# Exponentials as the stationary operand of the value products in a five-stream transformer kernel

## The reference

```
attn = jax.nn.softmax(jnp.einsum('bhqd,bhkd->bhqk', q, k) * scale, axis=-1)
out  = jnp.einsum('bhqk,bhkd->bqhd', attn, v).reshape(B, Lq, H)
x    = x + gate * (out @ Wp + bp)
```

## Time and profile before

| | |
|---|---|
| median of 3 runs | 2109.46 us (2109.4 to 2112.23) |
| profiled execution | 2114.21 us, span 2112.3 us |
| PE busy | 1954.2 us, 93% |
| PE weight loads busy | 1598.7 us |
| DVE busy | 1719.4 us, 81% |
| ACT busy | 1319.1 us, 62% |
| POOL busy | 832.2 us, 39% |
| mean granted TensorE clock | 0.988 of full speed |

### The profile page before, as it was taken

How to read it: one execution, slowest core, us unless ns; L and a number is a source line. 1 busy time by engine, 2 the same in 40 slices (tenths; PEclk the granted TensorE clock), 3 DMA queues, 4 the chain that set the end, 5 groups by cost and what they waited for, 6 DMA issues and landing times.

```text
span 2112.3 us, 93901 instructions
## 1 busy us (share of the span) xinstructions
PE 1954.2 (93%) x40741; PEld 1598.7 (76%) x40741; DVE 1719.4 (81%) x4395; ACT 1319.1 (62%) x3500; POOL 832.2 (39%) x1452
## 2 busy tenths in 40 slices
PE   3788999999999999999999999999999999999998
PEld 3566777787777787777787777887877877877777
DVE  2678788888788888789888889888889888889875
ACT  1344666676666676666666665676766666675666
POOL 1332343444343444343434343434443444344333
PEclk9899999999999999999999999999999999999999
DMA  4200000000000000000000000000000000000000
GB/s 164 56 2 3 15 20 21 8 16 20 21 20 21 8 18 18 21 20 21 8 21 18 18 21 21 20 9 20 18 18 21 21 20 8 21 15 8 3 3 14
DMA packets 48118, 43.01 MB, mean 20 GB/s; under 512 B 12640, under 2 KB 38368, under 8 KB 47456
## 3 DMA queue, kind: packets, MB, share of 16 engines
q1 hardware_dynamic: 47712, 37.02, 6.2%
HBM read 32.54 MB, written 4.46 MB: 18 GB/s over the span
## 4 chain that ended last, share of the span: by engine, by line
PE 60%; DVE 29%; issue 4%; ACT 3%; POOL 2%; DMA 1%; DVEq 0%; ACTq 0%; POOLq 0%
PE bank L975 9%; DVE top L1068 7%; PE bank L866 6%; PE bank L848 5%; PE bank L882 5%; PE bank L870 5%; DVE n_rows L1037 4%; PE bank L895 4%; PE bank L922 4%; DVE inv_sum L1072 4%; PE bank L912 4%; PE bank L905 3%; PE bank L786 3%; PE bank L819 3%; DVE q_heads L1059 2%
## 5 line engine op out<-in xcount | busy, mean ns | idle before, releaser
L724 POOL TENSOR_TENSOR shifted<-moments,eps 128x2 f32<-128x2 f32 x256 | 50.9, 199 | 1046.7 <-DVE moments L1031 1046.0
L1203 ACT ACTIVATE pT<-bank 128x512 f32<-128x512 f32 x640 | 330.4, 603 | 177.6 <-PE bank L870 177.3
L1068 DVE TENSOR_REDUCE top<-bank 128x8 f32<-128x512 f32 x640 | 394.7, 678 | 43.5 <-PE bank L848 42.0
L1072 DVE RECIPROCAL inv_sum<-bank 128x256 f32<-128x256 f32 x160 | 279.6, 1748 | 43.1 <-PE bank L882 42.9
L866 PE MATMUL bank<-inv_sum,of_keys 32*128 32x128 f32 x5120 | 278.9, 286 | 8.0 <-ACT inv_sum L1161 5.9
L870 PE MATMUL bank<-q_heads,k_heads 32*128 32x128 f32 x5120 | 262.7, 273 | 1.4 <-issue 1.1
L1037 DVE TENSOR_SCALAR n_rows<-x_rows,moments,rstd 128x128 f32<-128x128 f32 x512 | 198.4, 429 | 52.8 <-POOL rstd L726 52.1
L866 PEld LDWEIGHTS bank<-inv_sum,of_keys 32*128 32x128 f32 x5120 | 208.4, 188 | 40.8 <-ACT inv_sum L1161 26.5
L1238 ACT ACTIVATE pT<-bank,mod 128x64 f32<-128x64 f32 x896 | 194.7, 334 | 52.6 <-PE bank L975 51.5
L1180 ACT ACTIVATE k_heads<-bank,key_bias,own_head_sb 128x256 f32<-128x256 f32 x320 | 163.3, 563 | 96.6 <-PE bank L823 95.2
L870 PEld LDWEIGHTS bank<-q_heads,k_heads 32*128 32x128 f32 x5120 | 210.0, 189 | 2.5 <-issue 2.4
(11 more groups left out here) (147 smaller groups left out, 4044.4 us busy)
## 6 DMA issues: line engine op xcount, KB each, us to landing
gates<-gate_store SPq DMA_DIRECT2D x64, 256.0 KB, 4.1
x_rows<-x SPq DMA_DIRECT2D x32, 128.0 KB, 2.1
c_rows<-context SPq DMA_DIRECT2D x32, 128.0 KB, 2.1
out<-x_rows SPq DMA_DIRECT2D x32, 128.0 KB, 1.9
w_sb<-weights SPq DMA_DIRECT2D x1, 2368.0 KB, 12.8
pT<-weights SPq DMA_DIRECT2D x1, 1024.0 KB, 4.9
logit_bias<-logit_store SPq DMA_DIRECT2D x64, 1.5 KB, 3.4
row_sb<-rows SPq DMA_DIRECT2D x1, 769.5 KB, 6.8
```

The costliest lines, as they stand in the source:

```text
L1068: nc.vector.tensor_reduce(top[s][:, 32 * g:32 * g + 2 * GROUP], by_turn[g][:, :].rearrange("p (c k) -> p c k", k=SEQ), AX.X, ALU.max).then ...
L1072: nc.vector.reciprocal(inv_sum[s][:, :], banks.take()[:, 0:TOK]).then_inc(v_emptied, 1)
L1203: nc.scalar.activation(turn_cols[s][:, g, :], by_turn[g][:, :], ACT.Exp, scale=ATT_SCALE).then_inc(scores_read, 1)
```

## The change

1. **values**: pT becomes the stationary operand, 32 queries at a time (128x32), and two heads' v_heads of 9 columns each, 18 in all, move past it. Column 9 is all ones, so a head's sum stands beside its 8 outputs. 64 matmuls in the four column tiles instead of 32, and the step **sums** is gone. The matmuls of a turn wait for that turn's exponentials alone. Outputs have queries on the partitions.
2. DVE takes 128x32 reciprocals and multiplies them, broadcast over 8 features, into o_rows. A new step **heads** follows: PE transposes o_rows (two transposes, ring bank for ACT) and ACT moves them into oT.
3. **tops**: the four banks are one PSUM tensor; one TENSOR_REDUCE of 128x2048 waits for the last matmul of the step.
4. v_heads is written by two ACT copies of 64 partitions x 256 instead of four of 128.
5. The context's rows are normed by ACT, as c_rstd * c - mean * c_rstd (two ACTIVATEs of 128x128 with both operands by partition); POOL makes both norms' factors at once. POOL's expert-bias mix takes four wider instructions instead of ten.
6. low and the small attention's p3 and pn3 lie in o_rows instead of inv_sum, one DMA (own_ones) goes, and SEQUENCE is another string of the same length.

```diff
-    return [..., ("scores", None), ("sums", None), ("values", None), ("out", a)]
+    return [..., ("scores", None), ("values", None), ("heads", None), ("out", a)]
...
-        v_heads = each("v_heads", [D, GROUP * TURNS, 2 * QUAD])
+        v_heads = each("v_heads", [D, 2 * GROUP * TURNS, 2, HD + 1])
+        o_rows = each("o_rows", [D, 2, D])
+        inv_sum = each("inv_sum", [D, 2 * HEADS])
...
@@ PE
-                    if kind == "sums":
-                        after("pT", s)
-                        for lo in range(2):
-                            for g in range(TURNS):
-                                mm = nc.tensor.matmul(dst[QUAD * g:QUAD * (g + 1), 0:TOK], own_ones[:, lo, :], pT[s][:, g, :, lo, :],
-                                                      start=lo == 0, stop=lo == 1)
-                    if kind == "values":
-                        after("pT", s)
-                        for tb in range(GROUP):
-                            for lo in range(2):
-                                for g in range(TURNS):
-                                    mm = nc.tensor.matmul(dst[QUAD * g:QUAD * (g + 1), tb * SEQ:(tb + 1) * SEQ],
-                                                          v_heads[s][:, tb * TURNS + g, lo * QUAD:(lo + 1) * QUAD], pT[s][:, g, tb, lo, :],
-                                                          start=lo == 0, stop=lo == 1)
+                    if kind == "values":
+                        for g in range(TURNS):
+                            pe.wait_ge(scores_read, ready["pT", s] + g + 1)
+                            for t in range(2):
+                                for lo in range(2):
+                                    for b in range(2):
+                                        for half in range(2):
+                                            tb, at = 2 * t + b, SEQ * b + 32 * half
+                                            mm = nc.tensor.matmul(dst[at:at + 32, t, g, :, lo, :], pT[s][:, g, tb, lo, 32 * half:32 * half + 32],
+                                                                  v_heads[s][:, 2 * (tb * TURNS + g) + lo, :, :], start=True, stop=True)
+                    if kind == "heads":
+                        after("o_rows", s)
+                        transpose2(to_a.slot(), lambda t: o_rows[s][:, t, :], a_filled)
@@ DVE
-                        for g in range(TURNS):
-                            nc.vector.tensor_reduce(top[s][:, 32 * g:32 * g + 2 * GROUP], by_turn[g][:, :].rearrange("p (c k) -> p c k", k=SEQ), AX.X, ALU.max)
+                        nc.vector.tensor_reduce(top[s][:, :].rearrange("p (g c) -> p g c", c=32)[:, :, 0:2 * GROUP],
+                                                turns[:, :, :].rearrange("p g (c k) -> p g c k", k=SEQ), AX.X, ALU.max)
-                        nc.vector.reciprocal(inv_sum[s][:, :], banks.take()[:, 0:TOK])
-                        nc.vector.tensor_tensor(oT[s]..., src[:, 0:TOK], inv_sum[s][:, :], ALU.mult)
+                        own_result(nc.vector.reciprocal(inv_sum[s][:, :], src[:, :, HD]))
+                        nc.vector.tensor_tensor(o_cols[s]..., src[:, :, 0:HD], inv_sum[s][:, :].unsqueeze(2).broadcast_to([D, 2 * HEADS, HD]), ALU.mult)
@@ ACT
+                        for t in range(2):
+                            m = nc.scalar.activation(cn_rows[s][:, t, :], c_rows[s][:, t, :], ACT.Identity,
+                                                     scale=c_rstd[s][:, e, t:t + 1], bias=c_minus[s][:, e, t:t + 1])
+                    if kind == "heads":
+                        move(oT[s][:, :, :], bank4(banks.take()))
```

More of the change, by code:

```diff
@@ L134, in attention @@
     return [("q", a), ("k", a), ("v", a), ("tops", None), ("lows", None), ("scores", None),
-            ("sums", None), ("values", None), ("out", a)]
+            ("values", None), ("heads", None), ("out", a)]
 def mlp(m):
@@ L220, in bank_uses @@
         "kvnorm": (1, 0) if modulated else (0, 1), "q": (1, 0), "k": (0, 1), "v": (0, 1),
-        "lows": (0, 1), "sums": (1, 0), "values": (1, 0),
+        "lows": (0, 1), "values": (1, 0), "heads": (0, 1),
         "out": (1, 0), "fc1": (0, 1), "fc2": (1, 0), "l3_query": (0, 1), "l3_scores": (1, 0),
@@ L434, in build @@
         logit_store = nc.dram_tensor("logit_store", (B, EXPERTS), F32, kind="Internal").ap()
-        bank = [ctx.enter_context(nc.psum_tensor(f"bank{i}", [D, 512], F32)) for i in range(8)]
+        bank = [ctx.enter_context(nc.psum_tensor(f"bank{i}", [D, 512], F32)) for i in range(4)]
+        turns = ctx.enter_context(nc.psum_tensor("turns", [D, TURNS, 512], F32))
+        bank += [turns[:, g, :] for g in range(TURNS)]
         first_sem = sem("weights_in")
@@ L462, in build @@
         rows_normed, c_normed = [sem(f"rows_normed{s}") for s in range(STREAMS)], [sem(f"c_normed{s}") for s in range(STREAMS)]
-        c_moments_in = sem("c_moments_in")
+        c_moments_in, c_scaled = sem("c_moments_in"), [sem(f"c_scaled{s}") for s in range(STREAMS)]
         n_modulated = sem("n_modulated")
@@ L556, in _ @@
                 nc.gpsimd.memset(eps[:, TIGHT, :], 1e-6).then_inc(consts_made, 1)
-                nc.gpsimd.memset(minus_half[:, :], -0.5).then_inc(consts_made, 1)
+                nc.gpsimd.memset(minus_halves[:, :, :], -0.5).then_inc(consts_made, 1)
                 for s in range(STREAMS):
-                    nc.gpsimd.memset(v_heads[s][:, :, :], 0.0).then_inc(consts_made, 1)
+                    nc.gpsimd.memset(v_heads[s][:, :, :, :], 0.0).then_inc(consts_made, 1)
+                for s in range(STREAMS):
+                    pool.wait_ge(consts_made, 3 + STREAMS + 2 * s)
+                    for pair in range(2):
+                        nc.gpsimd.memset(v_heads[s][SEQ * pair:SEQ * (pair + 1), :, pair, HD:HD + 1], 1.0).then_inc(consts_made, 1)
             @block.tensor
@@ L1187, in _ @@
                             part = slice(SEQ * pair, SEQ * (pair + 1))
-                            for lo in range(2):
-                                at = lo * QUAD + (2 * pair + lo) * HD
-                                m = nc.scalar.activation(v_heads[s][part, :, at:at + HD],
-                                                         src[part, 0:TOK].rearrange("p (n l d) -> p n l d", l=2, d=HD)[:, :, lo, :],
-                                                         ACT.Identity)
+                            m = nc.scalar.activation(v_heads[s][part, :, pair, 0:HD],
+                                                     src[part, 0:TOK].rearrange("p (n d) -> p n d", d=HD), ACT.Identity)
                         m.then_inc(a_emptied, 1)
```

166 lines of the change are left out of this document (78 added, 88 removed).

## The result

| | before | changed |
|---|---|---|
| median | 2110.85 us (4 runs) | 2164.6 us (4 runs, 2161.56 to 2172.44) |
| ratio | 1 | 1.0256, 95% interval 1.0222 to 1.0289 |
| span of the profiled execution | 2112.3 us | 2159.6 us |

The change makes the kernel 2.6% slower; 1991 us was forecast. The page of the changed kernel answers to the earlier trace rows. The last line is the queue that carries instructions: packets, MB, share of 16 engines.

The account below looks back on a forecast made before the run. PE was taken to bound the kernel, with DVE close behind. From 2114.2 us, -88 for PE's products and -30 for waits gave 1996, and the median's 4.7 us lower made 1991 us; the 8 in 10 range was 1920 to 2075.

Parts of the forecast that it names:

- Part 1, products: PE's products with the exponentials: 1.12 us plus 0.22 for transposes replace 1.89 an attention, -88 us over 160.
- The rule that a load waits for the running matmul of its tile: Rival on PE's products: weight loads do not overlap their own tile's matmul, 77 us more, 2068 us; chance 0.06.
- wrong if L884 takes over 1.3 us an attention: Sign on the products' line: 128 records were expected in 1.0 to 1.1 us; over 1.3 refutes the forecast.
- Parts 2 and 3: Engine loads: DVE falls from 1719 to about 1480 us, ACT rises from 1319 to about 1470; neither counts by itself.
- Part 4: POOL loses 105.5 us of context rows and narrows its expert mix; PE waits for it almost nowhere, costed at nothing.
- Part 5: PE's waits: DVE's relief up to -75 us, late exponentials up to +86; -30 taken.
- D: Rival, tight exponentials: half of the 0.54 us is lost (43 us) and DVE's waits stay; 2064 us, chance 0.16.
- E: Rival: PE stands at each first product for late exponentials, 86 us, plus 38 for table loads; 2145 us, chance 0.06.
- The 0.54 us: Before the products: PE's wait an attention for the last turn's exponential, due at 2.4 us; 86 us over 160.
- B: Rival: DVE was a second bound; all 75 us of waits go and half as much again; 1909 us, chance 0.20.
- the sixth, no change: Rival: no change within what can be told, products at +37 us with DVE's waits gone; chance 0.02.
- the far end: Upper price of the products on PE: 14 ns a record, 1.79 us for 128, +37 us over 160 attentions.

Follow-up runs that it names:

- after_onewait: The changed kernel, but the products wait once for all four exponentials instead of turn by turn; 2260.9 us, 1.071 of the kernel before.
- wide_reciprocals: after_wide with 128x256 reciprocals as before the change, giving DVE 1.4 us an attention more; 2251.5 us, 1.065 of the kernel before.
- after_wide: The changed kernel with the value products' stationary operand 64 queries wide instead of 32, so 32 matmuls an attention; 2075.5 us, 0.982 of the kernel before.
- after_hybrid: The changed kernel with half of the value products 64 queries wide, seven changes of width an attention; 2147.4 us, 1.019 of the kernel before.
- before_newseq: The kernel before with the changed kernel's SEQUENCE string and nothing else changed; 2263.8 us, 1.074 of the kernel before.

## Why the prediction was wrong

**Part 1, products.** The size was nearly right. 7.9 ns a record was taken; at 1.20 us for the step less the change-over it is 8.5 (13 us over the program). The rule that a load waits for the running matmul of its tile would have made 1.6 us; the 1.20 us for 128x32 operands speak against it, as the earlier trace rows did. The step that failed is what the row was made to bear: the spacing in the earlier trace rows was measured over 32 records. I took it as a rate that lasts for 128 of them, 256 instructions, and did not ask where the instructions come from. The page before has the queue's row too (326 packets), and the 12 us of "issue" waits were there to be asked about. The prediction's own sign, "wrong if L884 takes over 1.3 us an attention", came true with the stops (1.88 on average) and not without them (1.20).

**The missing term** is 152.5 - 12.4 = 140 us of waits for instructions. The prediction had no term for it, and so put it at nothing. With it the forecast would have been 2131. Of the 34 us that are then left, 40 are busy time of PE that did not go, less 14 of idle time, and 8 are the median, which lies 3 us above the profiled run here where the forecast took it 4.7 below. PE's busy time fell by 48 us where 88 were forecast; 13 are the records' spacing. The rest has a likely part in the granted clock: after the first 160 us, which both kernels spend in part at half clock, it stands at 1.2 GHz for 100 us instead of 22 by the trace's record of the grants, and 78 us at half rate are worth up to 39. I did not test that by itself. Together 2112.3 + 140 - 48 - 41 (waits for DVE and ACT) = 2163, against a span of 2159.6.

**Parts 2 and 3** held: durations within 3%, except cn_rows (491 ns for 420) and v_heads (404 for 387); busy times within 35 and 20 us.

**Part 4** held: POOL fell to 655.8 us, and PE waited for it nowhere.

**Part 5**, -30 forecast, came out as -41: DVE's waits -32, ACT's -9. The fear of late exponentials (D, E) was unfounded while PE waits turn by turn; after_onewait shows what it would have cost. The 0.54 us came of two readings. Four exponentials were put at 4 x 0.603 = 2.41 us, but the busy time of that line is 330.5 us over 160 attentions, 2.07 us for four, since they overlap. And the one piece of order shown was near the tightest case: PE reaches the products 1.1 us after the last scores in the fastest tenth of the attentions and 1.8 in the median.

**The rivals.** The time is beyond E's 2145, but E's mechanism did not happen: none of the five was the one that did. B has something for it that the changed kernel does not show: in wide_reciprocals DVE's relief is worth far more than PE's waits for DVE before the change. The price of the sixth, no change, was added up wrongly: +37 at the far end less all 75 of DVE's waits is 38 us faster, and comes to nothing only with half of them. Two small slips change no sum: a column takes 0.86 ns by the row that is named for it, not 0.83, and v_heads saves 15 us by its two figures, not 17. The Trainium skill (Runtime: NRT & Kernel Launch, Instruction fetch mechanics) says that instructions are refilled in 16 KiB blocks of 256 over a DMA queue of the engine's own, and that the cost of crossing a block is mostly hidden. The first half agrees with the 16.4 KB packets and the block of 256. The second does not hold at this density: 109 of some 389 crossings cost 152 us.

## What to carry to other kernels

Count a matmul by its instructions too: an fp32 matmul is four of them (the traces show two loads and two matmuls for each), and here PE got at best 256 in some 3.3 us, 78 a us. A block of 256 that went by in some 2 us (the median ahead of the 109 stops) was enough to bring a stop, so little was in store. A step that turns long matmuls into twice as many short ones can save streaming time and lose more than that to the supply; widen the stationary operand, or mix widths in two solid runs, and look whether idle time put down to "issue" stands at one place in every block of 256 instructions. A rate read from a short burst is not a sustained rate.

## What the runs showed of the hardware

- 128x32 loads with 18-column matmuls in four column tiles: about 8.5 ns a record while supplied. 128x64 loads in two column tiles: 1.98 us for 64 records, 31 ns a record. No run shows why a record takes over three times as long there.
- A change of column-tile width between 32 and 64 costs 0.11 us: the products took 2.37 us with seven changes and 1.73 with one.
- Two packets of 256 instructions never started closer together than 3.23 us in eighteen traces, and at its 109 stops in the changed kernel PE resumed 1.2 to 1.6 us after a landing.
- The lowest mean clocks went with the most idle time of PE, whatever its cause: 0.953 and 0.956 (315 and 358 us idle), 0.964 (222, waits for DVE), 0.968 (254), against 0.986 to 0.988 where PE was idle for 96 to 158 us. It is no rule: after_wide and after_hybrid had 0.979 with about 100 us idle, before_newseq 0.978 with 279.
